# Last stage of a four-block network on one core: balancing chain split into two halves, the first begun inside the attention before it

## The reference, cut to what matters

```python
def sinkhorn_log(logits, num_iters=50, tau=0.1):
    Z = logits / tau                     # per row of x a 4 x 4 matrix
    def step(carry, _):
        u, v = carry
        u = -logsumexp(Z + v[..., None, :], axis=-1)
        v = -logsumexp(Z + u[..., :, None], axis=-2)
        return ((u, v), None)
    ...
    return exp(Z + u[..., :, None] + v[..., None, :])
# n = 4 streams of C = 128 columns in a row of x
x_norm = x * rsqrt(mean(x * x) + eps)
H_res_logits = (x_norm @ W_res.T) + H_res_base     # 16 per row
H_pre  = softmax(x_norm @ W_pre.T + H_pre_base)    # 4 per row
H_post = softmax(x_norm @ W_post.T + H_post_base)  # 4 per row
g = sigmoid(gate); H_res = (1 - g) * I + g * sinkhorn_log(H_res_logits)
y = einsum('btnc,btn->btc', x_streams, H_pre) @ W_branch
out = einsum('btij,btjc->btic', H_res, x_streams) + y * H_post
```

## Time and profile before

| | |
|---|---|
| median of 3 runs | 1498.83 us (1498.23 to 1500.56) |
| the profiled execution | 1495.79 us, its span 1494.0 us |
| busy, share of the span | TensorE 90%, VectorE 75%, ScalarE 45%, GpSimd 23% |
| last unit's statistics done | 1375.9 us |
| balancing, first to last instruction | 1386.2 to 1468.2 us |
| mixing, up to the last on VectorE | 1490.0 us |

### The profile page before, as it was taken

The page is one execution under the profiler, slowest core; times in us unless marked ns, Lnnn a source line. Parts: engine busy times, 40 slices in busy tenths (PEclk is TensorE's granted clock), DMA queues, the critical chain, the costliest instruction groups (busy, mean ns, idle before and its releaser), DMA issues.

```text
span 1494.0 us, 18658 instructions
## 1 busy us (share of the span) xinstructions
PE 1342.3 (90%) x6492; PEld 965.3 (65%) x6492; DVE 1120.0 (75%) x2045; ACT 675.4 (45%) x1405; POOL 336.6 (23%) x386
## 2 busy tenths in 40 slices
PE   7999999999998989969999988999999999999104
PEld 5665666566576658637888865777777777777102
DVE  4788898888888997986555575656666666577998
ACT  4777877787423533432222224443434434343104
POOL 1112112211164010232111031221312221212620
PEclk9999999999999999989999998999999999999557
DMA  5677988798810011243211210101101201000001
GB/s 220 168 179 178 239 223 194 171 233 211 220 54 1 1 57 43 47 89 79 73 56 52 100 43 10 62 29 43 71 29 43 71 29 43 0 1 1 0 0 57
DMA packets 37910, 127.74 MB, mean 86 GB/s; under 512 B 4944, under 2 KB 10960, under 8 KB 31680
## 3 DMA queue, kind: packets, MB, share of 16 engines
q1 hardware_dynamic: 26304, 83.38, 16.1%
q0 software_dynamic: 11520, 43.26, 15.2%
HBM read 72.63 MB, written 10.75 MB: 56 GB/s over the span
## 4 chain that ended last, share of the span: by engine, by line
PE 56%; DVE 24%; ACT 7%; DVEq 6%; issue 4%; DMA 1%; POOL 1%; POOLq 0%; SPq 0%
PE PS L150 11%; PE PS L152 11%; PE PS L151 11%; DVE AR L676 5%; PE PS L925 4%; PE PS L963 4%; ACT s_sb L606 2%; DVE AR L2649 2%; PE PS L949 2%; DVE AR L2638 2%; DVEq L666 2%; DVE AR L2645 2%; PE PS L535 2%; DVE AR L682 2%; PE PS L510 1%
## 5 line engine op out<-in xcount | busy, mean ns | idle before, releaser
L438 POOL DMA_DIRECT2D AR<-AR x76 | 73.7, 1084 | 336.5 <-DMA AR<-AR 147.4
L151 PE MATMUL PS<-R16r 128*128 128x512 f32 (+1 forms) x328 | 122.4, 373 | 0.0
L535 PE MATMUL PS<-R,PT 128*128 128x512 f32 x256 | 116.1, 597 | 3.6 <-DVE X L716 3.6
L152 PE MATMUL PS<-R16r 128*128 128x512 f32 (+1 forms) x312 | 119.2, 382 | 0.0
L510 PE MATMUL PS<-R,HT 128*128 128x256 f32 x512 | 116.5, 381 | 2.5 <-ACT R L595 2.5
L510 PEld LDWEIGHTS PS<-R,HT 128*128 128x128 f32 x512 | 94.9, 190 | 15.4 <-ACT R L595 4.0
L1083 ACT COPY AR<-PS 128x512 f32<-128x512 f32 x64 | 37.5, 586 | 145.9 <-PE PS L152 145.5
L606 ACT ACTIVATE s_sb<-PS,sm 128x64 f32<-128x64 f32 x256 | 77.9, 336 | 52.1 <-DVE sm L701 51.6
L150 PE MATMUL PS<-HTr,R16r 128*128 128x512 f32 (+1 forms) x240 | 91.1, 380 | 5.0 <-DVE R16r L190 2.9
L150 PE MATMUL PS<-R16r,HTr 128*128 128x512 f32 (+1 forms) x224 | 90.3, 403 | 0.0
L152 PE MATMUL PS<-HTr,R16r 128*128 128x512 f32 (+1 forms) x240 | 87.9, 366 | 0.0
(11 more groups left out here) (313 smaller groups left out, 3507.3 us busy)
## 6 DMA issues: line engine op xcount, KB each, us to landing
AR<-AR POOLq DMA_DIRECT2D x76, 528.0 KB, 6.8
OR<-in_wo SPq DMA_DIRECT2D x12, 1024.0 KB, 12.7
dequantised<-AR SPq DMA_DIRECT2D x8, 1056.0 KB, 5.5
WR<-in_w0q SPq DMA_DIRECT2D x8, 1024.0 KB, 11.4
AR<-in_w3q SPq DMA_DIRECT2D x8, 1024.0 KB, 4.9
WR<-dequantised SPq DMA_DIRECT2D x22, 256.0 KB, 2.7
AR<-in_nf SPq DMA_DIRECT2D x4, 1056.0 KB, 9.3
nf_in<-in_nf SPq DMA_DIRECT2D x4, 1056.0 KB, 9.0
```

The costliest lines, as they stand in the source:

```text
L151: nc.tensor.matmul(out, ah, bl, start=False, stop=False)
L152: return nc.tensor.matmul(out, al, bh, start=False, stop=last_)
L438: nc.gpsimd.dma_start(nf_below(g)[:, part], what[:, part], accum_op=ALU.add, max_dma_last_dim=4 * N_NF // 2).then_inc(added, 16)
L535: i = nc.tensor.matmul(bank(5 + tt), PT[:, at:at + P], vo[:, pr, b, :], start=pr == 0, stop=pr == 1)
```

## The change

The chain is cut into two halves h of four tiles (0: tiles 0 to 3, 1: tiles 4 to 7), each with buffers, a PSUM bank for the logits (7 and 4) and one for the kernels (6 and 5) of its own. A class `VectorF3` holds VectorE's pieces, and `dve_f3` is a written-out order of them. Half 0's logits, row maxima and row sums stand inside unit 31 of the attention; half 1's set-up stands between short runs of half 0's balancing; from there the two go in turns, each with its refresh while the other goes on (`renew`); half 0 comes to its mixing matrix 24 instructions before half 1. The branch is computed by halves. ScalarE with TensorE now mixes tiles 0, 1, 6, 7 (the first two as soon as half 0 has its matrix), GpSimd tile 3 and the first two streams of tile 2, VectorE tile 4, the other two streams of tile 2, and tile 5. Stores go in the order 0, 3, 1, 6, 2, 4, 7, 5. The table load and exponential of the gate move to the end of unit 29 on ScalarE, the constants to the end of unit 29 on VectorE. In unit 30 VectorE makes `probs_low` before the shift.

```diff
 def pe_x3(pe):              # in the loop over units
                 if u == NU0 - 2:
                     pe.wait_ge(A3["q_sq"], 2 * NU0)
                     pe_turn7(pe, 0)
                     pe_turn7(pe, 1)
-                    pe_turn7(pe, 2)
-                    pe_logits(pe, 0)
-                    pe_logits(pe, 1)
                 if u == NU0 - 1:
-                    pe.wait_ge(A3["s_read"], NU0)
-                    pe_turn7(pe, 3)
                     pe_turn7(pe, 4)
-                    pe_logits(pe, 2)
                     pe_turn7(pe, 5)
...
                 outputs(u, 1)
+                if u == NU0 - 2:
+                    pe_turn7(pe, 2)
+                    pe.wait_ge(A3["s_read"], NU0)
+                    pe_turn7(pe, 3)
+                    pe_logits(pe, 0)
 def act_x3(act):
                 if u == NU0 - 2:
-                    act_norm(act, 7, (0, 1, 2))
+                    act_norm(act, 7, (0, 1))
...
+                if u == NU0 - 3:
+                    nc.scalar.preload_act_table_set("natural_log_exp_and_others")
+                    nc.scalar.activation(SG[:, 0:1], gate[:], ACT.Exp, scale=-1.0).then_inc(F3["gate_exp"], 1)
+                if u == NU0 - 2:
+                    act_norm(act, 7, (2, 3))
-            act_norm(act, 7, (3, 4, 5))
-            nc.scalar.preload_act_table_set("natural_log_exp_and_others")
...
+            act_norm(act, 7, (4, 5))
+            act_rows(act, 0)
+            act_weights(act, 0)
+            act_logarithm(act, 0, 3)
 def dve_x3(dve, f3):
+                if u == NU0 - 2:
+                    probs_low(u)
                 if u + 1 < NU0:
                     shift(u + 1)
-                probs_low(u)
+                if u != NU0 - 2:
+                    probs_low(u)
+                if u == NU0 - 2:
+                    scaled7(dve, (0, 1))
+                if u == NU0 - 1:
+                    f3.logits(0)
+                    f3.rows(0)
...
-                if u == NU0 - 1:
-                    scaled7(dve, (2, 3, 4, 5))
...
                     nc.vector.bn_stats(st[:, T - 2, :], X[:, T - 2, :])
+                    f3.row_sums(0)
...
+                if u == NU0 - 3:
+                    f3.constants()
 def pool_f3(pool):
+            def mix(t, parts):
+                for j in range(NS):
+                    add_spread(t, hn_of(7, t)[:, j * P:(j + 1) * P], tiles(K3[0])[:, t, j:parts * NS:NS], parts)
+                pool.drain().then_inc(F3["done_pool"], 1)
+            ahead(0)      # waits for "post" of half 0: seven operations of 128x512, then one of 128x32
+            ahead(1)
+            behind(0)     # waits for "y_sb": for four tiles a multiply and an add
+            behind(1)
+            pool.wait_ge(F3["mixed"], 1)
+            mix(3, NS)
+            mix(2, 2)
 def act_f3(act):
+            act_norm(act, 7, (6,))
+            act_columns(act, 0)
+            act_norm(act, 7, (7,))
+            act_logarithm(act, 0, 5)
+            act_kernels(act, 0, 6)
...
+            branch(0)
+            branch(1)
...
+            weighted(0)
+            weighted(1)
+            mixed_tile(0)
+            weighted(2)
+            mixed_tile(1)
+            weighted(3)
+            mixed_tile(2)
+            mixed_tile(3)
 class VectorF3:
+            def balance(self, h, n):
+                for _ in range(min(n, self.limit[h] - self.done[h])):
+                    part = self.done[h] % ROUND
+                    k, given, got = (KP[h], CC[h], RR[h]) if part < 3 else (KT[h], RR[h], CC[h])
+                    self.after_last(h)      # waits for this half's previous instruction
...
 def dve_f3(dve, f3):
+            f3.columns(0)
+            scaled7(dve, (2, 3))
+            f3.column_sums(0)
+            scaled7(dve, (4, 5))
+            f3.shifted_columns(0)
+            f3.kernels_ready(0, 7)
+            def turns(h):
+                while f3.left(0) and f3.left(1):
+                    f3.balance(0, 1)
+                    f3.balance(1, 1)
+            def renew(h):
+                f3.factors(h)
+                f3.balance(1 - h, 6)
+                f3.refresh(h)
+                f3.balance(1 - h, 6)
+                f3.kernels_ready(h, 10)
+            f3.balance(0, 4)
+            scaled7(dve, (6, 7))
+            f3.balance(0, 4)
+            f3.logits(1)
+            f3.rows(1)
+            f3.balance(0, 3)
+            f3.row_sums(1)
+            f3.balance(0, 3)
+            f3.columns(1)
+            f3.balance(0, 3)
+            f3.column_sums(1)
+            f3.balance(0, 3)
+            f3.shifted_columns(1)
+            f3.balance(0, 4)
+            f3.kernels_ready(1, 7)
+            turns(0)
+            renew(0)
+            turns(1)
+            renew(1)
+            turns(0)
+            f3.mixing(0)
+            f3.balance(1, f3.left(1))
+            f3.mixing(1)
+            dve.wait_ge(F3["posted"], 2)
+            for group in (((4, 0), (2, 2)), ((5, 0),)):
...
```

More of the change, by code:

```diff
@@ L784, in dve_x0 @@
             dve_stats(dve, PAIRS - 1)
+        TH = T // 2
         PIECES3 = 10
@@ new lines, in ahead @@
+            def ahead(h):
+                pool.wait_ge(F3["post"], h + 1)
+                for n in range(NS):
+                    dst = XTMP if n else XP[h]
+                    nc.gpsimd.tensor_tensor(dst.rearrange("p (t c) -> p t c", t=TH), rows7(h)[:, :, n, :],
+                                            tiles(PP[h])[:, :, n].unsqueeze(2).to_broadcast([P, TH, P]), ALU.mult)
+                    pool.drain()
+                    if n:
+                        nc.gpsimd.tensor_tensor(XP[h], XP[h], XTMP, ALU.add)
+                        pool.drain()
+                pool.drain().then_inc(F3["pre"], 1)
+                nc.gpsimd.tensor_tensor(PP[h], PP[h], tg[:, 1, 3:4].to_broadcast([P, TH * 2 * NS]), ALU.mult)
+                pool.drain()
@@ new lines, in behind @@
+            def behind(h):
+                pool.wait_ge(F3["y_sb"], h + 1)
+                for k in range(TH):
+                    add_spread(TH * h + k, Y[h][:, k * P:(k + 1) * P], tiles(PP[h])[:, k, NS:2 * NS], NS)
+                pool.drain().then_inc(F3["posted"], 1)
+            def mix(t, parts):
+                for j in range(NS):
+                    add_spread(t, hn_of(7, t)[:, j * P:(j + 1) * P], tiles(K3[0])[:, t, j:parts * NS:NS], parts)
+                pool.drain().then_inc(F3["done_pool"], 1)
@@ new lines, in act_columns, with act_kernels, act_factors, branch @@
+        def act_columns(act, h):
+            act_asked(act, h, 4)
+            act_run(K3[h], Z[h], ACT.Exp)
+        def act_kernels(act, h, n):
+            act_asked(act, h, n)
+            act_run(KP[h], Z[h], ACT.Exp)
+            act_run(KT[h].rearrange("p (t j i) -> p t j i", t=TH, j=NS), matrices(Z[h]).rearrange("p t i j -> p t j i"),
+                    ACT.Exp)
+        def act_factors(act, h):
+            act_asked(act, h, 7)
+            act_run(RC[h], RC[h], ACT.Ln)
+        def act_f3(act):
+            def branch(h):
+                act.wait_ge(F3["preT_mm"], h + 1)
+                nc.scalar.copy(XPT[h], bank(3)).then_inc(F3["preT"], 1)
+                act.wait_ge(F3["y_mm"], h + 1)
+                nc.scalar.copy(Y[h], bank(3)).then_inc(F3["y_sb"], 1)
+            def weighted(k):
+                t = PE_TILES[k]
+                h = t // TH
+                act.wait_ge(F3["mixed"], h + 1)
+                for j in range(NS):
+                    for i_ in range(NS):
+                        i = nc.scalar.activation(products(k, j)[:, i_ * P:(i_ + 1) * P],
+                                                 hn_of(7, t)[:, j * P:(j + 1) * P], ACT.Copy,
+                                                 scale=tiles(K3[h])[:, t % TH, i_ * NS + j:i_ * NS + j + 1])
+                    i.then_inc(F3["prod_act"], 1)
@@ new lines, in mixed_tile @@
+                nc.scalar.copy(X[:, PE_TILES[k], :], bank(k)).then_inc(F3["done_act"], 1)
+            act_norm(act, 7, (6,))
[3 more added lines that the diff above has]
+            act_kernels(act, 0, 6)
+            act_rows(act, 1)
+            act_weights(act, 1)
+            act_logarithm(act, 1, 3)
+            act_columns(act, 1)
+            act_logarithm(act, 1, 5)
+            act_kernels(act, 1, 6)
+            branch(0)
@@ L2797, in _ @@
             dve_f2(dve)
-            dve_x3(dve)
-            dve_f3(dve)
+            f3 = VectorF3(dve)
+            dve_x3(dve, f3)
+            dve_f3(dve, f3)
 def lay_out(i):
```

500 lines of the change are left out of this document (238 added, 262 removed).

## The result

The changed kernel takes 1504.55 us (median of 10 runs, 1500.53 to 1509.32), the kernel before 1498.03 beside it (10 runs, 1495.62 to 1500.56): a ratio of 1.0046, 95% interval 1.0034 to 1.0058. It is slower by 6.5 us between the medians. The forecast, slower, 1507.3 with a range of 1500 to 1512, held. The profiled execution has a span of 1503.0 us; before's was 1494.0, and 1502.5 was forecast.

What follows compares the result with a forecast made beforehand. It priced the path of last statistics, set-up, VectorE's latency-bound balancing chain, mixing and stores: 0.7 + 8.9 - 4.9 + 4.6 - 0.8 = +8.5 us on 1498.83, giving 1507.3, range 1500 to 1512.

Steps and rivals of the forecast that it cites:

- Latency, not issue: Balancing chain: each instruction waits for its half's previous one; a half alone saves nothing, 49 iterations last 79 us however paired.
- C: From the first pair of the two halves to ScalarE's first mixing operation: 78.3 us for 83.2, -4.9.
- pace rival: Balancing chain: an instruction alone costs what a paired one does, 0.134 us; total +2.1, 1500.9 us; chance 0.06.
- Set-up: Last statistics to start of half 1's chain: 14.9 us without collisions, for 10.3 before.
- Collisions: VectorE's set-up operations with two SBUF operands, or wide one-operand copies, take turns with GpSimd by instruction: +4.3 us.
- The rival that they cost nothing: GpSimd gives way to VectorE or their times miss each other: +1.3 us in all, 1500.1; chance 0.17.
- deeper collisions: Every two-operand VectorE operation waits a whole GpSimd one, just one getting in behind each: 1511.6 us; chance 0.15.
- D: From ScalarE's first to VectorE's last mixing operation: 25.2 us, +4.6, behind ScalarE's 21.5.
- The last two units: Attention units 30 and 31, up to the last statistics: +0.7 us, taking half of a 1.3 us low-clock cost.
- A: From TensorE's scores of unit 31 to the end of the last statistics: +0.7 us.
- B: From the last statistics to the first pair of the two halves (before: first balancing instruction): +8.9 us.
- E: From VectorE's last mixing operation to the span's end: one store instead of two, -0.8 us.

Runs made afterwards that it cites:

- after: The changed kernel as described, against the kernel before: 1504.55 us, ratio 1.0046; profiled span 1503.0 us.
- half 0 alone: Changed kernel with half 1's balancing left out after its first six instructions: 1500.36 us, ratio 1.0016 to the kernel before.
- GpSimd held back: Changed kernel with GpSimd's half 0 work after half 1's column sums, its additions to X after the second refresh request: 1501.07 us, ratio 1.0017.
- before with late additions: Kernel before with GpSimd's additions to X held until ScalarE has been asked for the refresh: 1496.64 us, ratio 0.9990.
- gaps filled: Three cures, plus ten of half 0's lone balancing instructions put ahead of the drains of half 1's set-up: 1498.23 us, ratio 1.0003.
- the three cures: Changed kernel with GpSimd's branch work late, tile 2 wholly on VectorE, TensorE's eight sums over the weights in unit 30: 1499.15 us, ratio 1.0012.

## Why the prediction was right

**Latency, not issue.** Shown by the lone triples of after and of half 0 alone (0.80 us each), and by C, 78.19 for 78.3. The argument from the earlier trace rows held: once the second half starts later, nothing gives that back. The Trainium skill's rule (VectorE: DVE Perf Modes, The DRAIN you can't avoid), that the next operation waits until the pipe is empty, is not what the rows show, since paired operations of 64 elements overlap. The prediction cited it without the exception that stands in the same paragraph: a next operation that is not held starts earlier. With the exception the paragraph agrees with the rows, and gives the pace rival no support.

**Set-up.** 14.9 us by widths from the earlier trace rows, and 14.5 measured (14.86 with GpSimd held back, less the last shift's 0.38); so the base was 0.4 too high. Halving the width saved little, as priced: a 64-element multiply is 0.22 us, a 128-element one 0.29.

**Collisions.** +4.3 forecast, 4.4 in the rows, 4.06 and 0.29% by the experiment. The rival that they cost nothing falls, and the one of deeper collisions too: an operation waited for the rest of one GpSimd instruction, and ended 0.08 to 0.28 us behind it. Of half 1's logits one operation met GpSimd (0.67), not three (0.8); the shift of half 0 (0.85 for 0.7) made up for it. The Trainium skill says this more sharply on another page (SBUF — State Buffer, Who interferes with whom): the pair of ports is held for a whole instruction by whichever started first, and a reduction never contends. The rows agree: a reduction at 1395.67, with GpSimd busy from 1395.28 on, keeps its 0.22 us, while the shift beside it takes 0.60. The prediction's own word "wide" for the one-operand kind was wrong: the Trainium skill's section that it names (GPSIMD Engine Reference, Key points) speaks of a perf mode and of no width, and L2773, with 16 elements, waited too (1.07 us for 0.24).

**Mixing.** D was 24.88 for 25.2, with VectorE last, ScalarE at 21.59 (21.5) and GpSimd at 17.83 (17.5).

**The last two units.** Here a step was mis-sized, and its reasons were wrong. The prediction left `turn_p` of unit 31 "where it is", put `probs_low` 31 at 0.6 us sooner and the last statistics 6.6 us behind it for 5.7, which made +0.3, and then took half of a low clock. The two parts add up to 1.0 and not to the +0.7 that it entered, and its price of a low clock doesn't come out either (12 matmuls at 0.43 for 0.23 us are 2.4, not 1.3). The measured +1.17 has no low clock in it. Outputs 30 started 2.06 us sooner and took 1.54 less at the full clock (2.91 us for 4.45), but between them and `turn_p` of unit 31 stand 8 transposes and 40 narrow matmuls, where 20 had been counted, and they take 5.26 us: `turn_p` comes 5.26 - 2.06 - 1.54 = 1.66 late. Of that `probs_low` 31 sees 0.39, because in before it had waited for VectorE itself; the other 0.78 are VectorE's operations of half 0, near the 0.9 that these 6.6 us stand for. Eight of the narrow matmuls, moved out, gave back 0.9 us. That +0.7 came near +1.17 is luck in part: a low clock that didn't come stood in for a `turn_p` that was late.

**Stores.** -1.61 for -0.8: VectorE's last mixing operation was followed by 4.08 us in before and by 2.47 in after.

The five stretches together are +7.54 for +8.5: A 0.5 up, B and D 0.3 down each, C 0.1 down, E 0.8 down. Another 0.8 of the gap between 1507.3 and 1504.55 is the base: before's own median was that much lower in ten runs than in the three shown. The last 1.0 is between the marks and the medians, which are 6.5 and 7.1 us apart in the two measurements, and no row places it.

**What stays open.** What makes TensorE's clock fall in one unit or another was not settled. In the last two units it fell in outputs 30 in before and in before with late additions; in outputs 31 in the two kernels that put `probs_low` first into before's order; just ahead of `turn_p` of unit 31, and into outputs 31, in the profile without GpSimd's mixing and, for a shorter time, in the one with the gaps filled; and in none of the other seven profiles, all of the changed kernel or near it. It is not TensorE's waits alone: the profile without GpSimd's mixing has the same single wait of 0.92 us ahead of outputs 30 as after, and the same program up to there. With the three cures the changed kernel is still 2.0 us behind in A to E: +0.3 in A, +4.5 in B and +3.8 in D, for -5.0 in C and -1.6 in E. Whether E is shorter because one store and not two lies behind the last event was argued, not tried by itself; the profile without GpSimd's mixing fits it, with two stores and 3.85 us behind ScalarE's last copy.

## What to carry to other kernels

Before splitting a dependent chain to start one half early, ask whether the later half starts later: if the chain is bound by latency, its last start sets the end, and of a set-up of small operations each half costs three quarters of the whole. Look next at what the freed engine time is filled with: a GpSimd operation beside VectorE operations with two SBUF operands, or beside copies and scalar operations with one (not reductions), cost the rest of itself each time here, and delaying it past the short critical piece is a one-line cure that also gave 1.2 us by the marks in the kernel before, though the times there don't clear the noise. When totals spread by several microseconds, compare profiles from a mark in front of the change; the stretches that an edit left alone repeated to 0.05 us here, but for A, which moved by up to 1.9 us with TensorE's clock.

## What the runs showed of the hardware that was not expected

- A VectorE operation with a 16-element operand collides too: the addition to the diagonal, L2773, one operand from SBUF, took 1.07 us for 0.24 beside GpSimd. The price was in the forecast (1.6 us for half 1's preparation, 1.57 measured), but not in its rule.
- TensorE's low clock differs between executions of what is the same code up to there: the changed kernel and the one without GpSimd's mixing differ only behind the attention, and the second had the clock at 0.50 in unit 31 and an A of 21.95 us for 20.10. Where it fell on outputs, seven or eight of the 12 matmuls started 0.43 us apart for 0.23, and the 12 took 4.3 to 4.5 us for 2.9; in the profile with the gaps filled it was three.
- C is 78.18 or 78.19 us in seven profiles of kernels that share it, while in these the start of unit 31's scores ranged from 1355.1 to 1360.2 us.
